# Graph network kernel, edge stage: each edge product in two halves, one behind each sum

## The chip, the cores and the metric

The kernel runs on one core of one Trainium2 chip. Its engines are TensorE (PE; its weight loads are listed as PEld), VectorE (DVE), ScalarE (ACT), GpSimd (POOL) and SyncE (SP, which here only starts DMAs). Each engine takes its own instructions in order, and they meet through semaphores. The metric is the time of one execution on the device in microseconds; times given are medians over runs.

## The reference

Four steps, each added to the node features x (6250 nodes, 256 features): a graph convolution, a mixture of 6 experts, a second graph network with 106250 edges, and a mixture of 8 experts. The change is in the third:

```python
def mish(x):
    return x * jnp.tanh(jax.nn.softplus(x))
x = mish(node_features @ W_dense.T + b_dense)
y = mish(edge_features @ W_edge.T + b_edge)
msg = jax.nn.relu(x[src] + y)
agg = jax.ops.segment_sum(msg, dst, num_segments=node_features.shape[0])
rst = x + agg
return mish(rst @ W_out.T + b_out)
```

Edges are sorted by destination. All arithmetic is in fp32.

## The kernel before

The kernel is a row of stages; `stage_edges` makes the messages of the second graph network and sums them by destination. Edges are in segments of 512 (four tiles, CG = 4, of P = 128), six segments (SLOTS) to a step of the loop. The mish of the edge features of the even segments was already made in the graph convolution's stage and lies in DRAM; that of the odd ones is made here, so three (MISH) a step.

For one segment: GpSimd gathers the node rows of its 512 sources by four indirect DMAs (L1608) into `node[s]`. VectorE (`message`) writes a one-hot matrix `hot` of the destinations (L1694) and adds the edge's mish to the node rows, four instructions (L1702). ScalarE (`rectified`) applies the relu in place (L1655). TensorE (`segment`, L1621) multiplies messages by one-hot: two halves of the features, four tiles each, 16 instructions in the records, 64 columns each, into `ps_a[s % 2]`. VectorE (`add`, L1712) adds the result to the table of sums at the segment's window. These are "the sums" below.

For one odd segment's edge features: SyncE loads a tile of 512 KB (L1568). TensorE (`product`, L1631) multiplies it by the weights: four tiles, two halves of the features each, 16 instructions in the records, 256 columns each, into `ps_z[r]`, which holds all four tiles. VectorE (`mish_begin`) adds the bias (L1684) and clips (L1685). ScalarE (`factor`, in `mish_factor` at L918 to L921) runs four activations. VectorE (`mish_end`, L1689) multiplies, and that frees `ps_z[r]`. The result is the `q` that `message` reads for an odd segment.

The order on each engine is written out by hand. In a step TensorE runs sums 0 and 1, product 0, sums 2 and 3, product 1, sums 4 and 5, product 2. ScalarE runs rectified 0 and 1, factor 2, rectified 2 and 3, factor 0, rectified 4 and 5, factor 1. VectorE runs message 0, add 5 of the step before, mish_end 0, message 1, add 0, mish_begin 2, message 2, add 1, mish_end 1, message 3, add 2, mish_begin 0, message 4, add 3, mish_end 2, message 5, add 4, mish_begin 1. SyncE loads edge tiles and stored mish tiles in one queue, each load behind a semaphore that says its buffer is free. TensorE's loop runs 33 steps, one more follows with two products, and then a short tail of sums.

A product waits for its edge tile (`edge_in[r]`, which also counts the DMA) and for its accumulator (`z_free[r]`); its last instruction signals `z_done[r]`, for which mish_begin waits.

Of the kernel before, what the change touches and what calls it, by code (L numbers as in the profile page):

```python
# [26 lines left out]
CG = 4  # L27
# [60 lines left out]
def take(eng, semaphore, n=1):  # L88

    eng.wait_ge(semaphore, n)  # L90
    eng.sem_inc(semaphore, -n)  # L91
# [1441 lines left out]
def stage_edges(nc, c):  # L1533
# [3 lines left out]
    with ExitStack() as ctx:  # L1537
# [16 lines left out]
        neg_in, neg_free, edge_in, edge_free = per_r("neg_in"), per_r("neg_free"), per_r("edge_in"), per_r("edge_free")  # L1554
        z_done, z_free, z_ready, q_ready = per_r("z_done"), per_r("z_free"), per_r("z_ready"), per_r("q_ready")
# [5 lines left out]
        def load_passes(eng):  # L1561
            return eng.value_load(c.passes[0:1, 0:1], min_val=1, max_val=TW // W + 1)

        @block.sync
        def _(sp):
            def load_edges(i, r):
                take(sp, edge_free[r])
                sp.dma_start(edge[r][:], io["edge_t"][bass.ds(i * SLOTS + (2 * r + 1), 1)].rearrange("a p k e -> p (a k) e")).then_inc(edge_in[r], 16)  # L1568

            def load_mish(i, r):  # L1570
                take(sp, neg_free[r])
                sp.dma_start(neg[r][:], c.mish_d[bass.ds(i * MISH + r, 1)].rearrange("a p j d -> p (a j) d")).then_inc(neg_in[r], 16)

            sp.dma_start(we[:], io["l_we"]).then_inc(w_in, 16)
            sp.dma_start(bias[:], io["l_be"]).then_inc(w_in, 16)
            for r in range(MISH):
                sp.sem_inc(edge_free[r], 1)
                sp.sem_inc(neg_free[r], 1)
            with sp.Fori(0, load_passes(sp)) as k:
                for r in range(MISH):  # L1580
                    load_edges(0, r)
                for r in range(MISH):
                    load_mish(0, r)
                load_edges(1, 0)
                load_edges(1, 1)
                with sp.Fori(0, IT - 2) as i:
                    load_edges(i + 1, 2)
                    load_mish(i + 1, 0)
                    load_mish(i + 1, 1)
                    load_edges(i + 2, 0)  # L1590
                    load_mish(i + 1, 2)
                    load_edges(i + 2, 1)
                load_mish(IT - 1, 0)
                load_mish(IT - 1, 1)

            for t in range(0, NT, LATER):
                sp.dma_start(c.x[:, t:t + LATER, :], c.mixed_d[t * P:(t + LATER) * P, :].rearrange("(s p) d -> p s d", p=P)).then_inc(x_in, 16)
            sp.wait_ge(x_in, NT // LATER * 16)
# [15 lines left out]
        @block.tensor  # L1614
        def _(pe):
            def segment(s):

                take(pe, msg_ready)
                for m in range(KD):
                    for j in range(CG):  # L1620
                        last = pe.matmul(ps_a[s % 2][:, m, :], node[s][:, j, m * P:(m + 1) * P], hot[s % MISH][:, j, :],  # L1621
                                         start=j == 0, stop=j == CG - 1)
                last.then_inc(sum_ready, 1)

            def product(r):
                take(pe, edge_in[r], 16)

                take(pe, z_free[r])
                for j in range(CG):
                    for m in range(KD):  # L1630
                        last = pe.matmul(ps_z[r][:, j, :], edge[r][:, m, j * P:(j + 1) * P], we[:, m, :], start=m == 0, stop=m == KD - 1)  # L1631
                last.then_inc(z_done[r], 1)

            def step(products):
                for r in range(MISH):
                    segment(2 * r)
                    segment(2 * r + 1)
                    if r < products:
                        product(r)

            pe.wait_ge(w_in, 32)
            with pe.Fori(0, load_passes(pe)) as k:
                for r in range(MISH):
                    product(r)
                with pe.Fori(0, IT - 2) as i:
                    step(MISH)
                step(MISH - 1)
                for s in range(TAIL):
                    segment(s)
# [621 lines left out]
```

## Time and profile before

| | |
|---|---|
| median of 3 runs | 4377.48 us (4377.31 to 4378.98) |
| profiled execution, its own time | 4372.94 us |
| its span | 4371.1 us, mean granted TensorE clock 0.843 |
| busy share of the span | PE 81%, PEld 71%, POOL 61%, DVE 54%, ACT 43% |
| L1621 sums, whole stage | 3328 matmuls, 544.8 us busy, 250.5 us idle before them |
| L1631 products, whole stage | 1664 matmuls, 497.6 us busy, 8.5 us idle before them |
| L1655 rectification | 208, 1044 ns each |
| L1608 gathers | 832, 959 ns each |

The span is the time from the first to the last instruction. Busy times come from the records of one profiled execution. Idle time before a group is what its engine did not do just before the group's instructions. The granted clock is TensorE's, as a share of full speed; it has two levels, 2.4 GHz (1.00) and 1.2 GHz (0.50), so a value between them is a mean over a stretch that has both.

### The profile page before, as it was taken

The numbers are of one execution on the slowest core, as the hardware profiler recorded it, in microseconds if no ns is written. First come the engines' busy times: TensorE is split into PE (matmuls) and PEld (weight loads), VectorE is DVE, ScalarE is ACT, GpSimd is POOL, SyncE is SP. The second block draws the span as 40 slices with busy tenths as digits, with TensorE's granted clock in tenths as the row PEclk, the third lists the DMA queues.
The fourth block names the chain that finished last, engine by engine and source line by source line (L and its number), as shares of the span: only waits on it lengthen the run. The fifth ranks groups of instructions, "written<-read, shape, count | busy, mean of one in ns | idle before, by whom it ended". The sixth has DMA issues, their size and how long they took to land. (4 is left out here: it accounts for less than half of the span.)

```text
span 4371.1 us, 66370 instructions
## 1 busy us (share of the span) xinstructions
PE 3546.1 (81%) x17618; PEld 3124.4 (71%) x17618; DVE 2361.0 (54%) x6877; ACT 1875.4 (43%) x2892; POOL 2687.4 (61%) x2732
## 2 busy tenths in 40 slices
PE   4777776777469999999999688888888877659999
PEld 4666666666468888888888577777777776548887
DVE  6555555555534554544544466666666665762222
ACT  4444444444313343333334455555555554643333
POOL 3677777777577776776750566666666664353444
PEclk7777778877769999999999777777777776759999
DMA  6454455445522222222220455555555555244443
GB/s 182 150 163 158 153 163 158 154 155 160 167 66 65 67 71 62 69 67 61 70 59 24 153 174 175 178 175 172 175 173 174 173 174 172 80 140 98 96 97 63
DMA packets 263719, 555.91 MB, mean 127 GB/s; under 512 B 59438, under 2 KB 148209, under 8 KB 263406
## 3 DMA queue, kind: packets, MB, share of 16 engines
q0 software_dynamic: 114784, 245.67, 21.3%
q1 hardware_dynamic: 142174, 294.77, 19.8%
q10 hardware_dynamic: 6576, 13.36, 0.9%
q8 instruction: 73, 1.20, 0.1%
q14 instruction: 112, 0.92, 0.1%
HBM read 435.56 MB, written 119.88 MB: 127 GB/s over the span
## 5 line engine op out<-in xcount | busy, mean ns | idle before, releaser
L1608 POOL DMA_INDIRECT y_node<-node_table,src_sb x832 | 798.2, 959 | 573.5 <-issue 348.6
L1088 POOL DMA_INDIRECT x_gath<-hidden_table,src_sb x832 | 794.2, 955 | 361.8 <-issue 268.2
L481 POOL DMA_INDIRECT conv_gath<-support_table,src_sb x832 | 787.9, 947 | 270.7 <-issue 258.4
L1621 PE MATMUL y_pa<-y_hot,y_node 128*128 128x64 f32 x3328 | 544.8, 339 | 250.5 <-PEq L91 250.5
L1621 PEld LDWEIGHTS y_pa<-y_hot,y_node 128*128 128x128 f32 x3328 | 530.4, 252 | 284.2 <-issue 282.8
L609 PE MATMUL conv_pz<-conv_we,conv_edge 128*128 128x256 f32 x1680 | 511.3, 472 | 18.1 <-PEq L91 18.1
L600 PE MATMUL conv_ps<-conv_hot,conv_gath 128*128 128x64 f32 x1664 | 278.3, 329 | 280.8 <-PEq L91 158.9
L1631 PE MATMUL y_pz<-y_we,y_edge 128*128 128x256 f32 x1664 | 497.6, 465 | 8.5 <-PEq L91 8.5
L600 PEld LDWEIGHTS conv_ps<-conv_hot,conv_gath 128*128 128x128 f32 x1664 | 261.1, 240 | 316.1 <-issue 182.6
L609 PEld LDWEIGHTS conv_pz<-conv_we,conv_edge 128*128 128x128 f32 x1680 | 402.9, 246 | 92.9 <-issue 18.8
L1631 PEld LDWEIGHTS y_pz<-y_we,y_edge 128*128 128x128 f32 x1664 | 395.0, 244 | 79.1 <-issue 8.9
L918 ACT ACTIVATE conv_q<-conv_q 128x1024 f32<-128x1024 f32 x105 | 111.0, 1057 | 554.8 <-ACTq L91 554.8
L724 POOL DMA_INDIRECT out<-e_outs,e_node x112 | 175.0, 1562 | 278.0 <-POOLq L91 260.9
L918 ACT ACTIVATE y_q<-y_q 128x1024 f32<-128x1024 f32 x104 | 109.9, 1057 | 488.8 <-ACTq L91 488.8
L1171 PE MATMUL x_ph<-x_xt,x_w 128*128 128x256 f32 (+1 forms) x1296 | 296.3, 373 | 0.7 <-PEq L91 0.6
L1177 PE MATMUL x_pm<-x_hid,x_w 128*128 128x256 f32 (+1 forms) x1296 | 290.8, 369 | 2.0 <-PEq L91 1.9
L1184 PE MATMUL x_py<-x_w,x_mid 128*128 128x256 f32 x1176 | 282.0, 381 | 1.3 <-PEq L91 1.3
L1299 ACT ACTIVATE x_hid<-x_ph,x_b 128x256 f32<-128x256 f32 (+1 forms) x324 | 129.1, 449 | 338.9 <-ACTq L91 338.7
L1105 PEld LDWEIGHTS x_ps<-x_hot,x_gath 128*128 128x128 f32 x1664 | 221.4, 202 | 72.6 <-DMA x_gath<-hidden_table,src_sb 43.7
L1105 PE MATMUL x_ps<-x_hot,x_gath 128*128 128x64 f32 x1664 | 218.9, 282 | 59.8 <-DMA x_gath<-hidden_table,src_sb 38.8
L1177 PEld LDWEIGHTS x_pm<-x_hid,x_w 128*128 128x128 f32 x1296 | 232.5, 197 | 29.0 <-issue 2.9
L1655 ACT ACTIVATE y_node<-y_node 128x1024 f32<-128x1024 f32 x208 | 212.0, 1044 | 93.2 <-ACTq L91 91.9
(249 smaller groups left out, 5920.0 us busy)
## 6 DMA issues: line engine op xcount, KB each, us to landing
conv_edge<-in_edge_t SPq DMA_DIRECT2D x105, 512.0 KB
edge_mish_table<-conv_neg SPq DMA_DIRECT2D x105, 512.0 KB, 3.0
y_edge<-in_edge_t SPq DMA_DIRECT2D x104, 512.0 KB, 5.0
y_neg<-edge_mish_table SPq DMA_DIRECT2D x104, 512.0 KB
e_rows<-expert_rows SPq DMA_DIRECT2D x56, 272.0 KB, 3.3
conv_gath<-support_table,src_sb POOLq DMA_INDIRECT x832
x_gath<-hidden_table,src_sb POOLq DMA_INDIRECT x832
y_node<-node_table,src_sb POOLq DMA_INDIRECT x832, 3.0
```

The costliest lines, as they stand in the source:

```text
L481: pool.indirect_dma_start(gath[g % SLOTS][:, j, :], None, table[:, :], bass.IndirectOffsetOnAxis(ap=c.src[:, col:col + 1], axis=0),).then_ ...
L600: last = pe.matmul(ps[s % 2][:], gath[s][:, j, :], hot[half][:, at + j, :], start=j == 0, stop=j == CG - 1)
L609: last = pe.matmul(ps_z[r][:, j, :], edge[r][:, m, j * P:(j + 1) * P], we[:, m, :], start=m == 0, stop=m == KD - 1)
L918: link(act, act.activation(q, q, ACT.Exp), own)
L1088: pool.indirect_dma_start(gath[g % SLOTS][:, j, :], None, table[:, :], bass.IndirectOffsetOnAxis(ap=c.src[:, col:col + 1], axis=0),).then_ ...
L1105: last = pe.matmul(ps[n][:], gath[s][:, j, :], hot[half][:, at + j, :], start=j == 0, stop=j == CG - 1)
L1171: last = pe.matmul(ph[:, m, 0:width(u)], w_1[e][:, k, m * P:(m + 1) * P], xt[u % 2][:, k, 0:width(u)], start=k == 0, stop=k == KD - 1)
L1177: last = pe.matmul(pm[:, m, 0:width(u)], w_2[e][:, k, m * P:(m + 1) * P], hid[e % 2][:, k, 0:width(u)], start=k == 0, stop=k == KD - 1)
L1184: last = pe.matmul(py[:, s, :], mid[e % 2][:, k, s * P:(s + 1) * P], w_3[e][:, k, :], start=k == 0, stop=k == KD - 1)
L1608: pool.indirect_dma_start(node[g % SLOTS][:, j, :], None, c.t3[:, :], bass.IndirectOffsetOnAxis(ap=c.src[:, col:col + 1], axis=0),).then_i ...
L1621: last = pe.matmul(ps_a[s % 2][:, m, :], node[s][:, j, m * P:(m + 1) * P], hot[s % MISH][:, j, :], start=j == 0, stop=j == CG - 1)
L1631: last = pe.matmul(ps_z[r][:, j, :], edge[r][:, m, j * P:(j + 1) * P], we[:, m, :], start=m == 0, stop=m == KD - 1)
```

## The change

The product takes a second argument. Half 0 does tiles 0 and 1, half 1 tiles 2 and 3. The two waits stand ahead of half 0, the signal behind half 1. In a step, half 0 of product r follows sum 2r, half 1 follows sum 2r + 1. Ahead of the loop, both halves follow each other as before. Nothing else differs.

```diff
-            def product(r):
-                take(pe, edge_in[r], 16)
-
-                take(pe, z_free[r])
-                for j in range(CG):
+            def product(r, half):
+                if half == 0:
+                    take(pe, edge_in[r], 16)
+
+                    take(pe, z_free[r])
+                for j in range(half * CG // 2, (half + 1) * CG // 2):
                     for m in range(KD):
                         last = pe.matmul(ps_z[r][:, j, :], edge[r][:, m, j * P:(j + 1) * P], we[:, m, :], start=m == 0, stop=m == KD - 1)
-                last.then_inc(z_done[r], 1)
+                if half:
+                    last.then_inc(z_done[r], 1)
 
             def step(products):
                 for r in range(MISH):
-                    segment(2 * r)
-                    segment(2 * r + 1)
-                    if r < products:
-                        product(r)
+                    for half in range(2):
+                        segment(2 * r + half)
+                        if r < products:
+                            product(r, half)
 
             pe.wait_ge(w_in, 32)
             with pe.Fori(0, load_passes(pe)) as k:
                 for r in range(MISH):
-                    product(r)
+                    for half in range(2):
+                        product(r, half)
```

## Rows read from the trace of the kernel before

**Rows 1.** Groups by line, 2500 to 3700 us: count, busy, mean, idle before.
```profile
L1621 PE MATMUL y_pa<-y_hot,y_node 128*128 128x64 f32 x3184 | 517.7, 337 | 235.5 <-PEq L91 235.5
...
L1631 PE MATMUL y_pz<-y_we,y_edge 128*128 128x256 f32 x1568 | 470.2, 466 | 0.0
```

**Rows 2.** Waits, 2500 to 3700 us: total us, times, longest.
```profile
DVE messages_table L1712 <- DVEq L91: 243.0, 80, 4.5
```

**Rows 3.** Timeline of one period: start, duration (us), engine, line, operation, idle before.
```profile
3028.02 7.06 PE L1621 MATMUL y_pa<-y_hot,y_node 128*128 128x64 f32 x32 [4.25 <-PEq L91]
3032.09 0.29 DVE L1712 TENSOR_TENSOR messages_table<-messages_table,y_pa 128x128 f32 x1 [4.50 <-DVEq L91]
...
3040.03 1.04 ACT L1655 ACTIVATE y_node<-y_node 128x1024 f32<-128x1024 f32 x1
...
3040.11 1.22 DVE L1689 SCALAR_TENSOR_TENSOR y_q<-y_q,y_pz 128x1024 f32<-128x1024 f32 x1 [0.27 <-DVEq L91]
...
3041.21 1.97 PE L1621 MATMUL y_pa<-y_hot,y_node 128*128 128x64 f32 x16 [0.30 <-PEq L91]
...
3043.60 0.29 DVE L1712 TENSOR_TENSOR messages_table<-messages_table,y_pa 128x128 f32 x1 [0.15 <-issue]
...
3044.76 2.08 PE L1621 MATMUL y_pa<-y_hot,y_node 128*128 128x64 f32 x16 [1.58 <-PEq L91]
...
3046.63 5.29 PE L1631 MATMUL y_pz<-y_we,y_edge 128*128 128x256 f32 x16
...
3046.96 1.06 ACT L918 ACTIVATE y_q<-y_q 128x1024 f32<-128x1024 f32 x1 [2.34 <-ACTq L91]
...
3051.54 1.99 ACT L1655 ACTIVATE y_node<-y_node 128x1024 f32<-128x1024 f32 x2
...
3052.72 3.76 PE L1621 MATMUL y_pa<-y_hot,y_node 128*128 128x64 f32 x32 [0.80 <-PEq L91]
...
3055.11 0.29 DVE L1712 TENSOR_TENSOR messages_table<-messages_table,y_pa 128x128 f32 x1 [2.82 <-DVEq L91]
...
3055.92 0.33 SPq L1568 DMA_DIRECT2D y_edge<-in_edge_t  x1
...
3056.32 3.67 PE L1631 MATMUL y_pz<-y_we,y_edge 128*128 128x256 f32 x16
...
3063.06 1.99 ACT L1655 ACTIVATE y_node<-y_node 128x1024 f32<-128x1024 f32 x2
...
3064.24 7.06 PE L1621 MATMUL y_pa<-y_hot,y_node 128*128 128x64 f32 x32 [4.25 <-PEq L91]
```

**Rows 4.** Sum 0, 33 stretches: start:end, length, PE busy, clock, DMA share, GB/s.
```profile
2497.51:2499.47 1.96, 1.96 (x16) 1.00 0.43 121
...
3656.76:3658.73 1.97, 1.97 (x16) 1.00 0.36 92
sum 65.00, PE 64.92; mean PE 1.97
```

**Rows 5.** Sum 4, 33 stretches, the same columns.
```profile
2520.62:2524.06 3.44, 3.44 (x17) 0.53 0.26 76
...
3028.02:3031.67 3.65, 3.65 (x17) 0.50 0.24 72
...
3680.39:3683.15 2.76, 2.76 (x17) 0.68 1.07 348
sum 109.28, PE 109.22; mean PE 3.31
```

**Rows 6.** TensorE and its clock in stretches of the same period, the same columns.
```profile
3023.80:3028.00 4.20, 0.00 (x0) 0.76 0.41 129
...
3044.70:3046.50 1.80, 1.74 (x16) 0.99 0.61 189
3046.50:3050.00 3.50, 3.50 (x11) 0.52 0.94 346
3050.00:3056.60 6.60, 5.80 (x43) 1.00 0.34 101
```

## The prediction

> **What bounds the kernel now.** The diff touches only the edge stage, which runs one period 34 times; the second and the last begin their first sum at 2497.51 and 3656.76 us [rows 4]. I read the costliest lines of 2500 to 3700 us first. TensorE's sums (L1621) take 517.7 us of those 1200 and its products (L1631) 470.2 [rows 1]; with 235.5 us idle, all of it before sums, no engine is full. The waits say who is late: VectorE stands 243.0 us in front of the additions (L1712), 80 times, about twice in a period [rows 2]. So sums are late for VectorE, and something is late for the sums. The timeline of one period tells what [rows 3].
>
> I name the sums of a period s0 to s5 and the products p0 to p2. The order on TensorE today is s0 s1 p0 s2 s3 p1 s4 s5 p2. In the period from 3028.02 to 3064.24 us, s4 starts at 3028.02, its addition at 3032.09. Behind that addition VectorE begins a mish, ScalarE makes its factor, and only then, being in order, rectifies the messages of the next s0 (3040.03, 1.04 us); s0 starts at 3041.21. The same link follows s0: addition 3043.60, factor from 3046.96 (four activations), rectification 3051.54, s2 at 3052.72. And again: addition 3055.11, rectification 3063.06, s4 at 3064.24. So the period is three equal links, each "sum, addition, mish, factor, rectification, next sum". From start to start they took 13.19, 11.51 and 11.52 us; with the sums' own 3.65, 1.97 and 1.97 us taken off (a pair of sums at 3052.72 lasts 3.76, s2 is the first half of it; 1.97 as s0), each link is 9.54 us that no sum is part of. The period is therefore
>
> 3 x 9.54 + (s0 + s2 + s4) + lateness of TensorE = 28.6 + (s0 + s2 + s4) + lateness.
>
> Only these three sums count; s1, s3, s5 and the products lie beside the links, as long as TensorE has finished when the next link needs it. Between the first and the last s0 of the 33 read lie 32 periods: 36.23 us each [rows 4]. s0 takes 1.97 us in every one [rows 4]. s4 takes 3.65 in the period shown, 2.76 in the last, 3.31 on average over 33 [rows 5]. Taking s2 as 1.97, 28.6 + 1.97 + 1.97 + 3.31 = 35.85, so lateness is 0.38 us: in most periods s2 waits some tenths for p0 (0 in the period shown, where it starts 0.14 after its rectification of 1.04 ends).
>
> Why s4 is slow and s0, s2 are not is the granted clock. TensorE was idle from 3023.8 to 3028.0; the mean clock there is 0.76, so it fell from 2.4 to 1.2 GHz halfway, and s4 ran at 1.2 [rows 5, 6]. s2 follows p0 without a pause, p0 having brought the clock back: it began at half clock (0.52 from 3046.5 to 3050.0) and ended at full, which lasted through s2 and s3 [rows 6]. s0 follows p2 after 0.30 us [rows 3]. The 1.58 us pause behind s0 was enough for one more fall: 0.99 up to 3046.5, then 0.52 [rows 3, 6].
>
> **The change part by part.** It removes and adds no matmul, no DMA and no load. The order becomes s0 p0a s1 p0b s2 p1a s3 p1b s4 p2a s5 p2b. Waits on the edge tile and on the free accumulator move to the a-half, the signal to the b-half.
>
> *The waits that move.* p0a is wanted behind s0, at 3043.18. Its accumulator is freed by the end of the mish (L1689) at 3041.33, 1.85 us before [rows 3]. Its edge tile is asked for behind the bias step of the p0 before (3055.92 [rows 3] for the next period), over 20 us before the next s0 ends, and SP's order does not change. p1a and p2a are in the same place one and two links on. Cost nothing; if that cover went, the a-half would hold s1 back, which VectorE wants only after its next message.
>
> *Signals of the products.* p0b ends before s2, as p0 does; p1b and p2b end behind s3 and s5, as p1 and p2 do. The mish that takes a product begins behind the addition two sums later, so nothing waits. Zero.
>
> *The odd sums.* s1, s3, s5 come half a product later, 1.84 us at full clock (half of p1's 3.67) and 3.4 at half (1.84 x 3.65 / 1.97, an estimate). s5's addition is wanted only behind the next period's first message, s1's and s3's behind one message each. s3 is the tightest: at worst about 0.5 us late, and VectorE has 4.50 us spare in front of s4's addition [rows 3]. Zero, with 0.5 us a period as upper end.
>
> *s2 no longer behind p0.* With p0a already done, TensorE is free before the rectification. The lateness goes: -0.38 us a period.
>
> *The pauses.* This is the large term. Today's pauses are one of 4.2 us and two short ones. After the change each group "even sum, half, odd sum, half" runs without pause, then waits for the next link. At full clock a group is 1.97 + 1.88 + 3.67 = 7.5 us in a link of 9.54 + 1.97 = 11.5: a pause of 4.0. If it begins at half clock and recovers in its first half-product, it is 3.65 + 3.4 + 1.88 + 1.84 = 10.8 in 13.2: a pause of 2.4. So s0, s2 and s4 each stand behind 2.4 to 4.0 us of idleness, where only s4 does today. Each then costs between 1.97 (clock kept) and 3.65 (all at half clock) [rows 4, 5]. Today's case of such a pause is s4, 3.31 on average. The pauses to come are shorter and the fall came about 2.2 us into the pause shown, so more of a sum may be done before the fall; I take 3.15 for all three, nearest to s4's row. s0 and s2: +1.18 each; s4: -0.16.
>
> A late s0 is passed on in full: its addition began only 0.15 us after VectorE was ready for it [rows 3].
>
> Sum: -0.38 + 1.18 + 1.18 - 0.16 = +1.82 us a period, 28.6 + 9.45 = 38.05 against 36.23. Over 34 periods +62 us. The profiled execution took 4372.94 us (span 4371.1 and 1.84 around it) and would take 4435. The median of the runs is 4.54 us above it; the same added to 4377.48 gives 4439.5, say 4440.
>
> The Trainium skill, "TensorE: Matmul & The Clock Gate", section "HAM oscillation — how this bites in real kernels", says that a loop whose short matmul bursts are parted by waits of some microseconds drops to half clock at every wait and starts each burst cold. The row of s4 agrees in direction, since 3.31 is near 3.65, but it shows that part of a sum can still run at full clock. By that rule taken fully the time would be that of the first rival.
>
> **Rivals.** (1) *Every even sum runs wholly at half clock*: 28.6 + 3 x 3.65 = 39.55, +3.3 a period, +113: 4490. It decides from a fall that always comes before the pause ends. For it: s4 at 3.65 in the period shown. Against: s4 at 3.44 and 2.76 in others [rows 5].
>
> (2) *The clock does not come back.* In the rows p0 had to run about 3.4 us at half clock before the return, and a half-product is now just that long before a sum cuts in. Then TensorE is the bound: three pairs of sums at 7.06 [rows 3] and three products at 6.8 are 41.6 us a period, +5.3, +182: 4560. Against: the sums between are work too, and the clock stayed at full through s2 and s3.
>
> (3) *Faster: the even spread keeps the clock up.* Work is now spread in three equal groups, the long stretch of half clock around s4, s5 and p2 could vanish. If all three sums take 1.97 and lateness goes, the period is 34.5, -1.7, -59: 4319. It decides by whether the clock outlives a pause of 4.0 us. Against: it fell in one of 4.2 and because of one of 1.58 [rows 3, 6].
>
> (4) *It does nothing to the order that matters*: an a-half waits for its accumulator or edge tile, so that it runs where the whole did: 4377. Against: the 1.85 us of cover above.
>
> **How the numbers follow.** Forecast (even sums partly slow) 0.68; rival 1 0.12; rival 2 0.05; rival 3 0.10; rival 4 and mixtures that cancel 0.05. The forecast's own ends: one of the three spared and the others at 3.3 give 28.6 + 1.97 + 6.6 = 37.2, +33 in all, 4410; all at 3.5 give 39.1, +98, 4475. The range 4395 to 4495 takes in rival 1 and, below, the unknown of the odd sums and a second one nearly spared; it leaves out rivals 2 to 4. Within 0.2% is within 8.8 us, about what a measurement of this kernel can tell from no change, or 0.26 us a period. Faster 0.10 (rival 3), same 0.05 (rival 4), slower 0.85 (the rest).
>
> **What would show it.** The distance from one s0 to the next: near 38 us. s0 and s2 no longer 1.97 but spread between 2 and 3.65 at clocks of 0.5 to 0.9; three pauses of TensorE a period, each of 2.4 to 4 us, all before even sums; s2 starting about 9.5 us after s0's end, behind a pause and not behind p0; VectorE's wait before additions up from 243 us. Links that stay 9.54 confirm the frame. Wrong would be: s0 or s2 at 1.97 throughout, links that grow, or a wait on an edge tile.

## The result: slower by 1.1%, forecast 1.4%, and the profile after

The changed kernel takes 4425.74 us (median of 4, 4415.06 to 4431.28), the kernel before 4377.40 in the same comparison: ratio 1.0108, interval 1.0085 to 1.0132, +48 us. Forecast were 4440 and a range of 4395 to 4495. The profiled execution took 4431.16 us (span 4429.0), 58 above the one of before; forecast for it were 4435. The runs of the changed kernel spread over 16 us, and the profiled one is near their slow end, while that of the kernel before (4372.94) is at the fast end of its own: the medians' +48 is the better measure of the loss.

TensorE's timeline of one period after the change, from p0a to the s0 of the next period (p0a s1 p0b, s2 p1a s3 p1b, s4 p2a s5 p2b, s0; start, duration, engine, line, operation, idle before; L1632 is now the product):

```profile
2949.60 3.19 PE L1632 MATMUL y_pz<-y_we,y_edge 128*128 128x256 f32 x8
2952.63 1.89 PE L1621 MATMUL y_pa<-y_hot,y_node 128*128 128x64 f32 x16
2954.36 1.95 PE L1632 MATMUL y_pz<-y_we,y_edge 128*128 128x256 f32 x8
2959.35 3.65 PE L1621 MATMUL y_pa<-y_hot,y_node 128*128 128x64 f32 x16 [3.05 <-PEq L91]
2962.80 3.42 PE L1632 MATMUL y_pz<-y_we,y_edge 128*128 128x256 f32 x8
2966.05 1.90 PE L1621 MATMUL y_pa<-y_hot,y_node 128*128 128x64 f32 x16
2967.78 1.95 PE L1632 MATMUL y_pz<-y_we,y_edge 128*128 128x256 f32 x8
2972.55 3.61 PE L1621 MATMUL y_pa<-y_hot,y_node 128*128 128x64 f32 x16 [2.82 <-PEq L91]
2975.95 3.67 PE L1632 MATMUL y_pz<-y_we,y_edge 128*128 128x256 f32 x8
2979.45 1.90 PE L1621 MATMUL y_pa<-y_hot,y_node 128*128 128x64 f32 x16
2981.18 1.95 PE L1632 MATMUL y_pz<-y_we,y_edge 128*128 128x256 f32 x8
2985.70 3.14 PE L1621 MATMUL y_pa<-y_hot,y_node 128*128 128x64 f32 x16 [2.57 <-PEq L91]
```

Groups of sum, half, sum, half, each without a gap inside. In front of s2, s4 and the next s0 stand pauses of 3.05, 2.82 and 2.57 us. A group opens slow (s2 3.65, p1a 3.42) and closes fast (s3 1.90, p1b 1.95). In [rows 3] only s4 stood behind such a pause. From s2 to s4 it is 13.20 us, the link of 9.55 and the 3.65 of s2. The other engines in that link, from s2's addition to s4:

```profile
2963.42 0.29 DVE L1715 TENSOR_TENSOR messages_table<-messages_table,y_pa 128x128 f32 x1 [4.50 <-DVEq L91]
...
2966.78 1.06 ACT L918 ACTIVATE y_q<-y_q 128x1024 f32<-128x1024 f32 x1 [6.63 <-ACTq L91]
...
2971.36 1.99 ACT L1658 ACTIVATE y_node<-y_node 128x1024 f32<-128x1024 f32 x2
```

Addition, factor, rectification, next sum, as in [rows 3]: only the sum has grown. The even sums over 33 periods (start:end, length, PE busy, clock, DMA share, GB/s), s0 first, then the closing lines of s2 and of s4:

```profile
2500.24:2502.69 2.45, 2.45 (x16) 0.77 0.37 107
2538.60:2541.80 3.20, 3.19 (x16) 0.58 0.30 87
...
2649.82:2651.79 1.97, 1.97 (x16) 0.99 0.35 89
...
2723.81:2727.46 3.65, 3.65 (x16) 0.50 0.37 108
...
3709.86:3713.49 3.63, 3.63 (x16) 0.50 0.37 108
sum 102.09, PE 102.00; mean PE 3.09
```

```profile
sum 97.24, PE 97.15; mean PE 2.94
```

```profile
sum 103.28, PE 103.20; mean PE 3.13
```

s0 was 1.97 in every period [rows 4] and is now anything between 1.97 and 3.65, mean 3.09; s4 went from 3.31 [rows 5] to 3.13. From first to last s0 it is 1209.62 us over 32 periods: 37.80 each, against 36.23. The duration of a sum follows the granted clock of its stretch row by row: 1.97 at 0.99, 2.45 at 0.77, 3.65 at 0.50.

VectorE's wait in front of the additions (total us, times, longest; 2500 to 3700 us):

```profile
DVE messages_table L1715 <- DVEq L91: 280.0, 117, 4.5
```

It was 243.0 in 80 waits [rows 2]; now VectorE waits for the even sums, s0 among them, and in some periods for s1 or s3, at most 1.05 us, which delays no link. Nothing new waits: the products have no idle time before them (last column), as before [rows 1].

```profile
L1632 PE MATMUL y_pz<-y_we,y_edge 128*128 128x256 f32 x1520 | 512.0, 497 | 0.0
```

### The profile page after: what moved, and what is told of

Same layout as the page of the kernel before. It is cut to its first block and busy times, and to the rows that moved or that the text cites. A ratio compares the mean times of both kernels' runs of the same rounds, so it can differ in the third digit from the quotient of the medians.

```text
span 4429.0 us, 66370 instructions
## 1 busy us (share of the span) xinstructions
PE 3554.7 (80%) x17618; PEld 3122.1 (70%) x17618; DVE 2366.0 (53%) x6877; ACT 1878.0 (42%) x2892; POOL 2690.8 (61%) x2732
## 3 DMA queue, kind: packets, MB, share of 16 engines
q8 instruction: 72, 1.18, 0.1%
## 5 line engine op out<-in xcount | busy, mean ns | idle before, releaser
L1632 PE MATMUL y_pz<-y_we,y_edge 128*128 128x256 f32 x1664 | 558.6, 496 | 8.7 <-PEq L91 8.7
L1632 PEld LDWEIGHTS y_pz<-y_we,y_edge 128*128 128x128 f32 x1664 | 406.4, 256 | 78.1 <-issue 9.1
L1177 PEld LDWEIGHTS x_pm<-x_hid,x_w 128*128 128x128 f32 x1296 | 232.4, 197 | 28.6 <-issue 2.9
```

The lines of the kernel that those rows point to most:

```text
L1177: last = pe.matmul(pm[:, m, 0:width(u)], w_2[e][:, k, m * P:(m + 1) * P], hid[e % 2][:, k, 0:width(u)], start=k == 0, stop=k == KD - 1)
```

## The experiments

All compare with the kernel before on the same chip. "Pause" below is TensorE's idle time in front of a sum, from the end of its last matmul record to the start of the sum, as a mean over 32 periods.

**Whole products, other place.** Is it the halving, or where the pauses fall?

```diff
                 for r in range(MISH):
                     segment(2 * r)
-                    segment(2 * r + 1)
                     if r < products:
                         product(r)
+                    segment(2 * r + 1)
```

> No product is halved: each whole product stands behind the even sum (s0 p0 s1, s2 p1 s3, s4 p2 s5), so TensorE changes between sums and products as often as in the kernel before. Theory (the pauses in front of s0, s2 and s4 let the clock fall, and these three sums set the period): the three pauses are the same as in the changed kernel, so the even sums average 2.7 to 3.3 us, the period is 37 to 38.5 us and the time 30 to 75 us above before (ratio 1.007 to 1.017). Rival (halving itself costs: more changes between sums and products): as before, ratio 0.998 to 1.002, period 36.2.

Measured: 4424.04 us, ratio 1.0100 (1.0083 to 1.0116), the loss of the changed kernel, with no product halved. TensorE's timeline from s4 to the next s0:

```profile
2830.28 3.21 PE L1621 MATMUL y_pa<-y_hot,y_node 128*128 128x64 f32 x16 [2.66 <-PEq L91]
2833.29 5.80 PE L1631 MATMUL y_pz<-y_we,y_edge 128*128 128x256 f32 x16
2838.93 1.90 PE L1621 MATMUL y_pa<-y_hot,y_node 128*128 128x64 f32 x16
2843.04 2.40 PE L1621 MATMUL y_pa<-y_hot,y_node 128*128 128x64 f32 x16 [2.22 <-PEq L91]
```

The pause, the slow even sum and the fast odd sum are there, and the odd sum comes behind a whole product. Means of s0, s2, s4: 2.94, 3.07, 2.95 us; period 37.56. The loss is there without halving, so halving itself is not the cost; the pauses in front of the even sums are there too.

**Only p1 halved.** p0 and p2 go whole behind s1 and s5:

```diff
                     for half in range(2):
                         segment(2 * r + half)
-                        if r < products:
+                        if r < products and r == 1:
                             product(r, half)
+                    if r < products and r != 1:
+                        product(r, 0)
+                        product(r, 1)
```

> Only p1 is halved (s2 p1a s3 p1b); p0 and p2 stay whole behind the odd sums, as before. Theory of the pauses: s0 still follows p2 and s2 still follows p0, and in front of s4 there is the same pause as before, so s0 and s2 stay at 1.97 us, s4 near 3.3, period 36.2, ratio 0.998 to 1.002. Rival (each halved product costs the same): a third of the measured loss of 48 us, +16 us, ratio 1.0037.

Measured: 4376.83 us, ratio 0.9999 (0.9990 to 1.0008). s0 1.97, s2 1.92, s4 3.43, period 36.35. A halved product that opens no new pause costs nothing; the rival's 1.0037 is outside the interval.

**p0 and p2 halved.** The same edit with `r != 1` and `r == 1` exchanged.

> p0 and p2 are halved, p1 stays whole behind s3. Theory of the pauses: s0 and s2 now stand behind a pause of TensorE, s4 as before, so all three even sums average 2.8 to 3.2 us, the period is 37.3 to 38.1, the whole loss is there: +40 to +65 us, ratio 1.008 to 1.015. Rival (each halved product costs the same): two thirds of the loss, +32 us, ratio 1.0073.

Measured: 4419.24 us, ratio 1.0088 (1.0075 to 1.0100); the rival's 1.0073 lies just outside. The time is as the pauses had it, the sums are not: I expected all three near 3, and over 33 periods s0 is slow (3.64), s2 is slow (3.25) and s4 fast (1.97). TensorE's timeline from s0 to s4, one of the 7 periods in which s2 itself was still fast (1.97 of the pair's 5.37) and s3 slow, and the closing line of s2 over 33 periods:

```profile
2873.95 3.65 PE L1621 MATMUL y_pa<-y_hot,y_node 128*128 128x64 f32 x16 [4.25 <-PEq L91]
2877.39 3.73 PE L1632 MATMUL y_pz<-y_we,y_edge 128*128 128x256 f32 x8
2880.91 2.73 PE L1621 MATMUL y_pa<-y_hot,y_node 128*128 128x64 f32 x16
2883.47 1.95 PE L1632 MATMUL y_pz<-y_we,y_edge 128*128 128x256 f32 x8
2887.14 5.37 PE L1621 MATMUL y_pa<-y_hot,y_node 128*128 128x64 f32 x32 [1.73 <-PEq L91]
2892.30 5.65 PE L1632 MATMUL y_pz<-y_we,y_edge 128*128 128x256 f32 x16
2898.66 1.97 PE L1621 MATMUL y_pa<-y_hot,y_node 128*128 128x64 f32 x16 [0.71 <-PEq L91]
```

```profile
sum 107.45, PE 107.40; mean PE 3.25
```

s3 and much of p1, and in 26 of 33 periods most or all of s2, run slow and so fill their link: s4 comes behind 0.71 us here, 1.03 on average, and is at full clock, 1.97 in every period. The group behind it is then fast too, and the longest pause, 4.24, is now in front of s0: 3.64 or 3.65 in every period. Halving p0 and p2 moved the old slow place from s4 to s0 and made s2 slow as well (3.25). Period 37.54.

**Pauses filled, too much.** The changed kernel, and the kernel before, with matmuls made again, over themselves, in their pauses:

```diff
                 if half:
+                    for again in range(7):
+                        for m in range(KD):
+                            last = pe.matmul(ps_z[r][:, CG - 1, :], edge[r][:, m, (CG - 1) * P:CG * P], we[:, m, :], start=m == 0, stop=m == KD - 1)
                     last.then_inc(z_done[r], 1)
```

> The changed kernel, in which the last tile of each product is made eight times instead of once before its signal: 14 more matmuls of 256 columns, 3.2 us at full clock, in each pause of 4 us. Theory of the pauses: the clock stays at full, all three even sums take 1.97 us, the period is 28.6 + 5.9 = 34.5 us, and the time is some 60 us below before (ratio 0.984 to 0.990) and 108 below the changed kernel, with 42 matmuls a period more. Rival (TensorE's work or its changes between sums and products are the cost): 42 matmuls more make it slower still, ratio over 1.011.

Measured: 4484.38 us, ratio 1.0238 (1.0222 to 1.0255). For the kernel before, tiles 0 to 2 of p0 are made once in advance behind s0 and the last tiles 3, 7 and 7 times again (`ready` holds the two waits of a product, `tiles` its loop; lines left out are marked ...):

```diff
+            def product(r):
+                tiles(r, range(CG))
+                tiles(r, [CG - 1] * (3, 7, 7)[r]).then_inc(z_done[r], 1)
...
                     segment(2 * r)
+                    if r == 0 and products:
+                        ready(0)
+                        tiles(0, range(3))
                     segment(2 * r + 1)
```

> The kernel before with its order and its whole products, and matmuls made again in its pauses: three tiles of p0 behind s0 (6 matmuls), the last tile of p0 three times more, that of p1 and of p2 seven times more. Theory of the pauses: with the clock at full, s4 takes 1.97 us too, and the period is 34.5 us as in the filled halves: equal to that kernel within 0.3%, ratio to before 0.984 to 0.990. Rival (halving costs in itself): this one is some 48 us faster than the filled halves.

Measured: 4451.01 us, ratio 1.0163 (1.0147 to 1.0180). Both times were missed, by my own size: one fp32 matmul of the program is two records (the 14 of the filler are 28 below), so the filler was twice as long as meant. Filled halves, TensorE's timeline of one group and the next sum:

```profile
2901.71 1.89 PE L1621 MATMUL y_pa<-y_hot,y_node 128*128 128x64 f32 x16
2903.44 1.95 PE L1632 MATMUL y_pz<-y_we,y_edge 128*128 128x256 f32 x8
2905.22 1.89 PE L1621 MATMUL y_pa<-y_hot,y_node 128*128 128x64 f32 x16
2906.95 1.95 PE L1632 MATMUL y_pz<-y_we,y_edge 128*128 128x256 f32 x8
2908.74 6.21 PE L1636 MATMUL y_pz<-y_we,y_edge 128*128 128x256 f32 x28
2914.78 1.89 PE L1621 MATMUL y_pa<-y_hot,y_node 128*128 128x64 f32 x16
```

There is no pause and the clock never falls, but a group is 13.07 us long (2901.71 to 2914.78) where the link with a fast sum is 11.5: TensorE is the bound, 3 x 13.07 = 39.2 a period. What the two show all the same: with no pause every sum takes 1.89 to 1.95 us, in either order.

**Pauses filled, the right size.** The filler of the halves cut from 7 to 4 repeats (16 records), that of the whole products from 3, 7, 7 to 2, 4, 4, and one tile behind s0 in place of three.

> The changed kernel with the last tile of each product made five times, not eight: each of its matmuls is two records, so the former filler was 28 records and 6.05 us, longer than the pause, and TensorE itself set the period of 39.2 us. Now 16 records, 3.45 us, in a pause of 4.0. Theory of the pauses: the clock stays at full, the even sums take 1.97, TensorE is done 0.5 us before each link ends, the period is 34.5, -59 us, ratio 0.984 to 0.990. Rival (the extra work or the changes between sums and products cost): slower than before, ratio over 1.003.

> The kernel before with its order and whole products, and shorter fillers: one tile of p0 behind s0 (4 records, 0.9 us, in a pause of 1.6), the last tile of p0 twice more (8 records, 1.7 us), that of p1 and p2 four times more (16 records, 3.45 us). Theory of the pauses: clock at full, s4 at 1.97, period 34.5, equal to the filled halves within 0.3%, ratio to before 0.984 to 0.990. Rival (halving costs in itself): this one is some 48 us faster than the filled halves.

Measured: filled halves 4321.97 us, ratio 0.9875 (0.9856 to 0.9894), -58 us and the fastest kernel here; filled whole products 4355.27 us, ratio 0.9948 (0.9934 to 0.9963). Filled halves, one group:

```profile
2901.75 1.97 PE L1621 MATMUL y_pa<-y_hot,y_node 128*128 128x64 f32 x16 [0.80 <-PEq L91]
2903.56 1.95 PE L1632 MATMUL y_pz<-y_we,y_edge 128*128 128x256 f32 x8
2905.34 1.90 PE L1621 MATMUL y_pa<-y_hot,y_node 128*128 128x64 f32 x16
2907.07 1.95 PE L1632 MATMUL y_pz<-y_we,y_edge 128*128 128x256 f32 x8
2908.85 3.62 PE L1636 MATMUL y_pz<-y_we,y_edge 128*128 128x256 f32 x16
2913.27 1.97 PE L1621 MATMUL y_pa<-y_hot,y_node 128*128 128x64 f32 x16 [0.80 <-PEq L91]
```

A pause of 0.80 remains, all even sums are 1.97 in all 33 periods, the period is 34.55: 28.6 + 3 x 1.97. 48 more records of 256 columns a period make the kernel 58 us faster than before and, by the two ratios, some 100 faster than the changed one. That settles the cause: what the changed kernel lost, the clock took.

The filled whole products came out 33 us slower, where I expected equality and the rival expected them faster. Their timeline from s4 on, a pair of sums that went well (s4 and s5, with p2 behind them and s0 of the next period), and then s2 and s3 of that next period, in which the clock fell:

```profile
2881.04 3.76 PE L1621 MATMUL y_pa<-y_hot,y_node 128*128 128x64 f32 x32 [0.80 <-PEq L91]
2884.63 7.13 PE L1628 MATMUL y_pz<-y_we,y_edge 128*128 128x256 f32 x32
2892.55 1.97 PE L1621 MATMUL y_pa<-y_hot,y_node 128*128 128x64 f32 x16 [0.80 <-PEq L91]
...
2904.07 4.76 PE L1621 MATMUL y_pa<-y_hot,y_node 128*128 128x64 f32 x32 [0.75 <-PEq L91]
2908.62 3.73 PE L1628 MATMUL y_pz<-y_we,y_edge 128*128 128x256 f32 x8
```

In 13 of 33 periods the clock fell in s3 (its mean is 2.34 us), though s2 stood behind only some 0.75 us; p1 and its filler then start slow and s4 is late, 36.85 us for that period against 34.55. These 13 make 30 of the 33 us. Two sums in a row behind a short pause do not explain it alone: s4 and s5, behind 0.80 us in the same kernel, stayed at full clock in every period. What differs ahead of s2 is a second pause, 0.67 us between s0 and s1, and the filler ahead (8 records behind p0, where s4 has 16 behind p1); which of the two counts is not shown. In the filled halves, with a half-product between the sums and one pause in each link, no sum was slow. So with these fillers the order of the change is the better one; an equal filler for both orders was not tried.

**One pause filled.** The changed kernel with the filler behind p0b alone:

```diff
                 if half:
+                    for again in range((4, 0, 0)[r]):
...
                     last.then_inc(z_done[r], 1)
```

> The changed kernel with a filler in one pause alone, the one in front of s2 (the last tile of p0 made five times; 16 records, 3.45 us). Theory of the pauses: s2 goes to 1.97 us, s0 and s4 stay near 3.1, the links stay 9.54, the period is 36.6 to 36.9, ratio to before 1.002 to 1.006. Rival (the clock is a matter of the work in a whole period, so a third of the filler lifts all three sums by a third): s0, s2 and s4 each near 2.7, period 36.7, told apart by s0 and s4 in the trace. Rival (extra work costs): slower than the changed kernel.

Measured: 4428.71 us, ratio 1.0113 (1.0096 to 1.0130). The closing lines over 33 stretches of s0, s2 and s4:

```profile
sum 91.70, PE 91.61; mean PE 2.78
```

```profile
sum 62.55, PE 62.49; mean PE 1.89
```

```profile
sum 120.36, PE 120.26; mean PE 3.64
```

s2, now mostly without a pause, is at full clock in every period and s4, behind a pause, in none: the clock belongs to what stands just in front, not to the work of the whole period. The mean of s0 alone would fit that rival; it is made of periods, mostly by turns, of 1.97 behind a pause of about 1.8 us and of 3.65 behind 3.1. The time was missed. Behind the fast s2 its whole group is fast and ends early, so the pause in front of s4 is 4.25, as in the kernel before, and s4 is 3.64 in place of 3.1. And the filler runs past the end of its link, since s0 or the half-product behind it still runs slow in nearly every period: the link from s0 to s2 is 10.10 on average in place of 9.54. Period 37.53, hardly below 37.80, so the time cannot tell this kernel from the changed one; that extra work is not in itself the cost rests on the filled halves.

## Why the prediction was right

- *The frame*, three links of 9.54 us plus the three even sums plus lateness: holds. After the change the links from s0 to s2, s2 to s4 and s4 to s0 (from start to start, the sum's own duration taken off, mean of 32) are 9.54 to 9.55 each; 28.6 + 3.09 + 2.94 + 3.13 = 37.8, the measured period.
- *The lateness of s2 goes, -0.38*: the link from s0 to s2 was 9.93 on average with p0 in it and is 9.54, -0.39.
- *The pauses*: forecast 2.4 to 4.0 us, measured 2.65, 2.48 and 2.82 before s0, s2 and s4 on average. *s0 and s2 +1.18 each, s4 -0.16*: measured +1.12, +1.03 (against its own 1.91, and +0.97 against the 1.97 that the sum used) and -0.18. The mean even sum was taken as 3.15 and is 3.05: the one term of the sum that was off. That it came so near is partly luck, since 3.15 was chosen next to s4's row between 1.97 and 3.65, and not worked out. In sum +1.57 a period, not +1.82. From the stage's first product to its last sum the profiled execution lost 53 us, not 62; of the other 5 of its 58 us, 1.7 come ahead of the stage and 2.9 behind it, where the diff changes nothing.
- *Readings of the rows that were off, without touching the sum*: [rows 3] show three short pauses, not two (0.30, 1.58, 0.80). s2 follows p0 without a pause in most periods, but stood behind 0.80 us in the one shown; s0's pause was 0.30 there and is 1.00 on average, 1.72 at most, with s0 at 1.97 always. The fall in s1 was put down to the 1.58 us behind s0 alone; the last section shows that the pause in front of s0 counts too.
- *Costs put at nothing* (waits moved, odd sums later, signals): no idle time before any product, and the links stay 9.54, so the odd additions delay none.
- *Rival 1, even sums wholly slow*: single periods only (three of 32 above 39.5 us, 39.55 at most), mean 3.05 and not 3.65. The rule of the Trainium skill that stood beside it ("TensorE: Matmul & The Clock Gate", section "HAM oscillation — how this bites in real kernels") has the direction and, taken fully, overstates the size here: bursts did not all begin cold (s0 took 1.97 at 0.99 in one of the periods shown). In the page's own case the burst is shorter than the wait behind it; here TensorE works over 7 us between two pauses of 2.5 to 2.8 us on average.
- *Rival 2, no return of the clock*: every b-half in the trace took 1.95 us, as at full clock.
- *Rival 3, faster by an even spread*: its price was right, 4319 forecast and 4322 with filled pauses, its condition was not: an even spread leaves long pauses. In the three of 33 periods in which the whole group of s2 ran fast, the pause behind it was 4.25 us, and s4 took 2.65.
- *Rival 4, no change of order*: s1 follows p0a without idle time.

What stays open is the size for one run: the clock's falls strike each sum at another point, the changed kernel's runs differ by 16 us, and only one of them was traced.

## What to carry to other kernels

Where a chain through other engines sets the period, ask which TensorE bursts lie on it, and what TensorE did just before each: the same burst costs 1.97 us behind a product that ended at full clock and up to 3.65 behind a long pause (or 3.62 right behind a slow sum, as s5 of the kernel before). Spreading TensorE's work evenly can make it slower, since it turns one long pause into several, here of 2.5 to 2.8 us on average, each still long enough. If the engine has time to spare, work made twice in the pause is a cheap way to keep the clock, but size it from records and not from the program's instruction count, and leave the chain its slack.

## What the runs showed of the hardware

Idle time in front of a sum and the sum's mean, over the kernels: 4.25 us and 3.31 (s4 before), 4.24 and 3.64 (s0 with p0 and p2 halved), 2.48 to 2.82 and 2.94 to 3.13 (the changed kernel), 1.03 and 1.97 (s4 with p0 and p2 halved), 0.80 and 1.97 (filled halves). Taken one by one, over 33 periods of each trace here, the sums that stood right behind a product kept the full clock (1.97 us) behind every pause from 0.1 to 1.91 us, 366 of them. Behind 1.97 to 2.1 us they took 2.0 to 2.2, behind 2.9 to 3.3 us 3.64 or 3.65, and behind 4.24 to 4.28 us anything from 2.59 to 3.65.

The pause in front does not decide alone. In the kernel before, s1 stands right behind s0, its pause is nearly the same in every period (1.28 to 1.62 us), and yet it takes 1.97 to 3.65 us, 3.14 on average: the more, the longer the pause in front of s0 was. It took 1.97 in the one period where that was 0.17, 2.08 in [rows 3] where it was 0.30, 3.64 or 3.65 where it was 1.20 or more, and here, where it was 0.65, 2.73 (s0, then s1):

```profile
3004.38 1.97 PE L1621 MATMUL y_pa<-y_hot,y_node 128*128 128x64 f32 x16 [0.65 <-PEq L91]
...
3007.92 2.73 PE L1621 MATMUL y_pa<-y_hot,y_node 128*128 128x64 f32 x16 [1.57 <-PEq L91]
```

I had not expected that a pause of 0.75 us could be followed by a fall at all, as in the filled whole products; there, too, another pause stood ahead of it.
